# Last layer's output stage: ScalarE scales every fourth chunk, GpSimd the other three

## What is computed

```
def _L3_conv_ref(z, ...):
    zn = _layernorm(z, ln_in_w, ln_in_b)
    a = jax.nn.sigmoid(zn @ Wga + bga) * (zn @ Wla + bla)
    b = jax.nn.sigmoid(zn @ Wgb + bgb) * (zn @ Wlb + blb)
    k = jnp.einsum('bimc,bmjc->bijc', a, b)
    out = jax.nn.sigmoid(zn @ Wgo + bgo) * (_layernorm(k, ln_o_w, ln_o_b) @ Wlo + blo)
    return out

x = x + _L3_conv_ref(_gn(x), ...)
```

## Time and profile before

| what | value |
|---|---|
| median of three executions | 2137.73 us (2136.56 to 2138.88) |
| profiled execution, its own time | 2139.81 us |
| its span in the trace | 2137.9 us |
| mean granted clock of PE, share of full speed | 0.961 |
| busy in the whole span: PE, DVE, ACT, POOL | 1773.6, 1526.9, 1309.6, 806.5 us |
| output stage of layer 3 | about 1985 us to the end |

### The profile page before, as it was taken

How to read it: one execution, slowest core, us unless ns; L and a number is a source line. 1 busy time by engine, 2 the same in 40 slices (tenths; PEclk the granted TensorE clock), 3 DMA queues, 4 the chain that set the end, 5 groups by cost and what they waited for, 6 DMA issues and landing times. The chain is left out here.

```text
span 2137.9 us, 40855 instructions
## 1 busy us (share of the span) xinstructions
PE 1773.6 (83%) x10389; PEld 1036.9 (48%) x10389; DVE 1526.9 (71%) x3171; ACT 1309.6 (61%) x2413; POOL 806.5 (38%) x740
## 2 busy tenths in 40 slices
PE   0899996797998999965699799877699997799665
PEld 0345444685553454543355476633344444588332
DVE  7588886126754999996876487488588889344775
ACT  0587884466995878754599576433378876344322
POOL 0045445006980444445799100188100000000799
PEclk9999998898999999998899899999899999899999
DMA  7367776775994456546499687299547877753799
GB/s 319 124 201 232 243 240 208 276 308 180 362 368 144 139 166 188 166 139 239 156 367 363 223 292 239 68 389 403 191 143 232 247 225 228 255 235 157 254 352 338
DMA packets 336161, 512.92 MB, mean 240 GB/s; under 512 B 23851, under 2 KB 189486, under 8 KB 329654
## 3 DMA queue, kind: packets, MB, share of 16 engines
q1 hardware_dynamic: 336054, 511.71, 69.4%
HBM read 293.51 MB, written 205.52 MB: 233 GB/s over the span
## 5 line engine op out<-in xcount | busy, mean ns | idle before, releaser
L1300 POOL TENSOR_TENSOR shared<-O,out_rs 128x128 f32<-128x128 f32 (+1 forms) x128 | 91.6, 718 | 678.2 <-DVE out_rs L1207 677.1
L599 PE MATMUL ps<-w_heads,hi 64*128 64x256 f16 x3072 | 290.8, 272 | 33.8 <-DVE sig L750 21.7
L662 ACT ACTIVATE sig<-ps,largest 128x512 f32<-128x512 f32 x384 | 247.3, 691 | 52.1 <-PE ps L599 49.3
L1097 ACT ACTIVATE O<-ps 128x512 f32 (+1 forms) x144 | 151.6, 1053 | 190.4 <-PE ps L1018 190.4
L1344 PE MATMUL ps<-ident,shared 128*128 128x128 f32 (+1 forms) x1024 | 162.9, 284 | 106.8 <-POOL shared L1300 106.7
L1344 PEld LDWEIGHTS ps<-ident,shared 128*128 128x128 f32 (+1 forms) x1024 | 114.2, 133 | 277.0 <-POOL shared L1300 192.2
L599 PEld LDWEIGHTS ps<-w_heads,hi 64*128 64x128 f16 x3072 | 154.0, 94 | 187.9 <-DVE sig L750 71.5
L643 ACT ACTIVATE zs<-ps,shift 128x512 f32<-128x512 f32 x192 | 131.8, 686 | 184.0 <-PE ps L567 183.8
L599 PE MATMUL ps<-w_heads,lo 64*128 64x256 f16 x1536 | 212.4, 270 | 0.0
L750 DVE SCALAR_TENSOR_TENSOR sig<-ps,largest,sig 128x512 f32<-128x512 f32 x256 | 179.6, 741 | 37.9 <-ACT sig L662 36.4
L567 PE MATMUL ps<-xs,center 128*128 128x512 f32 x384 | 202.8, 610 | 1.0 <-DVE shift L347 1.0
(11 more groups left out here) (156 smaller groups left out, 3718.6 us busy)
## 6 DMA issues: line engine op xcount, KB each, us to landing
shared<-left_right SPq DMA_DIRECT2D x34, 2048.0 KB, 12.1
shared<-gate SPq DMA_DIRECT2D x256, 256.0 KB, 4.5
gate<-gates SPq DMA_DIRECT2D x96, 512.0 KB, 2.9
x_dram<-shared SPq DMA_DIRECT2D x192, 256.0 KB, 4.3
shared<-x_dram SPq DMA_DIRECT2D x192, 256.0 KB, 4.6
xs<-x_dram SPq DMA_DIRECT2D x64, 512.0 KB, 4.2
left_right<-stage SPq DMA_DIRECT2D x64, 448.0 KB, 5.8
left_right<-shared SPq DMA_DIRECT2D x64, 448.0 KB, 5.8
```

The source lines that it names most:

```text
L599: last = pe.matmul(PAIR[row][:, g, kb * S:kb * S + S], tokens[half, q % 8, at:at + P], k["w_heads"][half, part, :], start=(step == 0), sto ...
L662: act.activation(sig[:, slot, :].rearrange("p (c e) -> p c e", c=4), pair(row, 0), ACT.Sigmoid, scale=k["largest"][:, 0:1]).then_inc(c["si ...
L1097: act.activation(o_of(ch), ps[h % 4 // 2][:, h % 2, :].rearrange("p (b g i) -> p b g i", b=2, g=2), ACT.Copy).then_inc(c["o_copied"].sem, 1)
```

## The change

In layer 3 alone (`shares_scale = n == 3`) the chunks whose number has remainder 3 modulo 4 are no longer scaled by POOL. ACT scales them, in a new `scale`: eight activations of 128x64, one for each group of tokens, with function Copy and the token's reciprocal as the per-partition scale operand. ACT does this for chunk q+4 right after its `copy` of chunk q+3. A new counter `act_scaled` tells PE when such a chunk is ready and DVE when the reciprocals may be overwritten; POOL's counter `scaled` now counts three chunks in four. Everything else, and layers 0 to 2, stay as they are.

```
--- before.py
+++ after.py
@@ -91,7 +91,7 @@
             "fold_vec", "fold_mm", "fold_act", "stat_done", "z_done", "sq_done", "var_done", "log_done", "r_done", "r_part", "r_split", "spread_done",
             "xn_done", "hi_done", "lo_done", "proj_done", "gate_mm_done", "sig_done", "gate_done", "masked", "lr_done", "pair_read",
             "tr_done", "tr_copied", "tri_done", "packed", "o_copied", "o_stored", "o_moved",
-            "ln_stat", "ln_root", "ln_scale", "centered", "scaled", "wt_done", "wt_copied", "gated",
+            "ln_stat", "ln_root", "ln_scale", "centered", "scaled", "act_scaled", "wt_done", "wt_copied", "gated",
             "out_mm_done", "u_cleared", "out_gated", "x_new", "counted", "aggregated")}
 
         for n, ring in (("const_in", 1), ("x_in", 8), ("lr_out", 2), ("first_out", 2), ("gate_out", 4), ("lr_in", 2),
@@ -1122,6 +1122,7 @@
     STAT, CENTER, SCALE, TURN, GATED, OUTMM, OUTGATED = BATCH + 6, 5, 4, 3, 2, 1 if gate_first else 2, 1
     LOAD_X, LOAD_G = 4, 6 if gate_first else 5
     RING = 4
+    shares_scale = n == 3
     with ExitStack() as ctx:
         def sb(name, shape, dt=F32):
             return ctx.enter_context(nc.sbuf_tensor(f"out_{name}_{n}", shape, dt))
@@ -1142,6 +1143,16 @@
             at = q % BATCH * 2 * ROWS
             return values[:, q // BATCH % BATCHES, :, at:at + 2 * ROWS, :].to_broadcast([P, 2, 2 * ROWS, H])
 
+        def scaled_by_act(q):
+
+            return shares_scale and q % BATCH == BATCH - 1
+
+        def scaled_by_pool(i, q):
+
+            if shares_scale:
+                return c["scaled"]((i * BATCHES + q // BATCH) * (BATCH - 1) + q % BATCH + 1)
+            return c["scaled"](i * BODY + q + 1)
+
         def bodies_of(eng, step):
 
             with eng.Fori(0, bodies - 1) as i:
@@ -1203,7 +1214,10 @@
                 batch = i * BATCHES + b
                 dve.wait_ge(c["ln_root"].sem, c["ln_root"](batch + 1))
 
-                dve.wait_ge(c["scaled"].sem, c["scaled"](batch * BATCH - (BATCHES - 1) * BATCH))
+                freed = batch - (BATCHES - 1)
+                dve.wait_ge(c["scaled"].sem, c["scaled"](freed * (BATCH - 1 if shares_scale else BATCH)))
+                if shares_scale:
+                    dve.wait_ge(c["act_scaled"].sem, c["act_scaled"](freed))
                 dve.reciprocal(rs[:, b % BATCHES].rearrange("p b t -> p (b t)"), std[:, b % BATCHES]).then_inc(c["ln_scale"].sem, 1)
                 dve.wait_ge(c["ln_scale"].sem, c["ln_scale"](batch + 1))
 
@@ -1313,7 +1327,7 @@
             def step(i, q, more):
                 if gate_first and more(CENTER):
                     center(i, q + CENTER)
-                if not gate_first and more(SCALE):
+                if not gate_first and more(SCALE) and not scaled_by_act(q + SCALE):
                     scale(i, q + SCALE)
                 if gate_first:
                     if more(SCALE):
@@ -1328,14 +1342,18 @@
                         scale(0, q - (CENTER - SCALE))
             else:
                 for q in range(SCALE):
-                    scale(0, q)
+                    if not scaled_by_act(q):
+                        scale(0, q)
             bodies_of(pool, step)
 
         @block.tensor
         def _(pe):
             def turn(i, q):
                 m = i * BODY + q
-                pe.wait_ge(c["scaled"].sem, c["scaled"](m + 1))
+                if scaled_by_act(q):
+                    pe.wait_ge(c["act_scaled"].sem, c["act_scaled"](i * BATCHES + q // BATCH + 1))
+                else:
+                    pe.wait_ge(c["scaled"].sem, scaled_by_pool(i, q))
                 free = c["gated"] if gate_first else c["wt_copied"]
                 pe.wait_ge(free.sem, free(m - 3))
                 for row in range(ROWS):
@@ -1386,6 +1404,18 @@
                     ins = act.activation(u[0:HH, q % RING], TURNED[q % 4], ACT.Copy)
                 ins.then_inc(c["wt_copied"].sem, 1)
 
+            def scale(i, q):
+                m = i * BODY + q
+                act.wait_ge(c["ln_scale"].sem, c["ln_scale"](i * BATCHES + q // BATCH + 1))
+                act.wait_ge(c["wt_done"].sem, c["wt_done"](m - 3))
+                for jb in range(2):
+                    for token in range(2 * ROWS):
+                        tokens = rows[:, jb, bass.ds(m * 2 * ROWS + token, 1), :].rearrange("p t h -> p (t h)")
+                        at = q % BATCH * 2 * ROWS + token
+                        last = act.activation(scaled[:, q % RING, jb, token, :], tokens, ACT.Copy,
+                                              scale=rs[:, q // BATCH % BATCHES, jb, at:at + 1])
+                last.then_inc(c["act_scaled"].sem, 1)
+
             def root(i, b):
                 batch = i * BATCHES + b
                 act.wait_ge(c["ln_stat"].sem, c["ln_stat"](batch * BATCH + BATCH))
@@ -1397,6 +1427,8 @@
             def step(i, q, more):
                 if more(TURN):
                     copy(i, q + TURN)
+                if more(SCALE) and scaled_by_act(q + SCALE):
+                    scale(i, q + SCALE)
                 if gate_first:
                     m = i * BODY + q
                     act.wait_ge(c["out_mm_done"].sem, c["out_mm_done"](m + 1))
@@ -1415,6 +1447,8 @@
                 act.wait_ge(c["u_cleared"].sem, c["u_cleared"](1))
             for q in range(TURN):
                 copy(0, q)
+            if shares_scale:
+                scale(0, SCALE - 1)
             bodies_of(act, step)
 
     for s in range(RING):
@@ -1427,7 +1461,10 @@
         c[name].advance(batches)
     if gate_first:
         c["aggregated"].advance(5)
-    for name in ("ln_stat", "scaled", "wt_done", "wt_copied", "out_mm_done", "x_new",
+    c["scaled"].advance(NCH - batches if shares_scale else NCH)
+    if shares_scale:
+        c["act_scaled"].advance(batches)
+    for name in ("ln_stat", "wt_done", "wt_copied", "out_mm_done", "x_new",
                  *(("centered", "gated") if gate_first else ("out_gated",))) + (("counted",) if counted else ()):
         c[name].advance(NCH)
 
```

## The result

| | before | changed |
|---|---|---|
| median of four executions each | 2137.62 us (2136.56 to 2138.88) | 2125.49 us (2124.29 to 2126.74) |
| profiled execution | 2139.81 us | 2126.74 us |
| its span | 2137.9 us | 2124.9 us |

The ratio is 0.9943, with a 95% interval of 0.9926 to 0.9960: 12.1 us less, 9 to 16 by the interval. The forecast was 2123.9 us, 13.8 less. A second set of executions of the changed kernel gave 0.9937 (0.9924 to 0.9950). Three executions in the whole series, of 2469, 2483 and 4650 us, lie far outside the others and are left out of all medians and ratios here.

The account below looks back on a forecast made before the run. POOL was taken to bound layer 3's output stage. Profiled 2139.8 us, less 15.0 for freed spacings, plus 1.2 for transfers, gives 2126.0; the median lies 2.1 below the profiled one, so 2123.9, range 2121.0 to 2130.5.

Parts of the forecast that it names:

- POOL sets the pace: Layer 3's output stage: POOL is busy 120.00 of 120 us, 2.23 us a chunk, and stays slowest after the change.
- 15 spacings of 1.00 us: POOL, layer 3's output stage: 15 of ACT's 16 chunks each free one multiplication spacing of 1.00 us, 15.0 in all.
- the last additions: End of layer 3's output stage: POOL's four back-to-back additions, 4.93 us from 2128.20, were to stay as they are.
- Transfers cost 1.2 us: Layer 3's output stage: imperfect meshing with transfers costs 0.02 us on each of 60 chunks; bounds 0 and 3.2 us.
- Eight activations take 1.6 us: ACT's scaling of one chunk: 7 spacings of 0.17 us plus a last activation of 0.39; bounds 1.35 and 3.1.
- the loop: PE's transposes, ACT's copy and scaling, then three PE steps: 6.9 us per four chunks, under POOL's 7.92.
- The threshold at which the loop decides: The loop through ACT becomes the pace and the change loses once eight activations need more than 3.6 us.
- the rival of the slow activations: Activations of 0.50 us each make the loop 9.3 us; 15 fours lose 0.4 each, 6 us, 2143.7; 4 in 100.
- PE gets denser work: PE in layer 3's output stage: full clock is granted in the stage before and work gets denser, so nothing changes.
- The limit of 358 GB/s: Skill's limit for HBM transfers of a core; the stage, at 354, would gain nothing, 2137.7 us; rival's chance 5 in 100.
- layer 2's rate of 398 GB/s: Layer 2's output stage, same three transfers per chunk: its rate shows the new pace of 397 GB/s is just possible.

Follow-up runs that it names:

- 16 columns of x: Changed kernel whose loads of x in the last output stage bring 16 of 512 columns: 2124.0 us, ratio 0.9930.
- twelve: Changed kernel with four extra activations, into an unread buffer, ahead of the eight at each of ACT's chunks: 2144.9 us, ratio 1.0025.
- the sixteen activations: Changed kernel with eight extra activations, into an unread buffer, ahead of the eight at each of ACT's chunks: 2172.3 us, ratio 1.0150.
- the filling: The sixteen activations, with PE also multiplying constants while it waits for ACT: 2154.7 us with twenty matmuls, 2142.6 us with fourteen.

## Why the prediction was right

- **POOL sets the pace: right.** The kernel before with a third of its transfers gone had the same time, and less or earlier work on ACT changed nothing.
- **15 spacings of 1.00 us: right, 14.2 arrived in the steady part.** From the start of the first addition to that of chunk 60 the kernel before took 132.7 us (1996.75 to 2129.4, the second of the four at 2128.20). The prediction took these four for the last additions; in the kernel before one more comes after them:

```profile
2134.16 1.26 POOL L1311 TENSOR_TENSOR shared<-shared 128x512 f32<-128x512 f32 x1 [1.03 <-DMA out<-shared]
```

In the changed kernel the same stretch, to chunk 60, takes 118.4 us, as POOL's timeline shows:

```profile
1997.14 1.26 POOL L1325 TENSOR_TENSOR shared<-shared 128x512 f32<-128x512 f32 x1 [1.43 <-DVE shared L1238]
...
2011.16 1.27 POOL L1325 TENSOR_TENSOR shared<-shared 128x512 f32<-128x512 f32 x1 [0.38 <-DMA out<-shared]
...
2115.59 1.27 POOL L1325 TENSOR_TENSOR shared<-shared 128x512 f32<-128x512 f32 x1 [0.16 <-DMA out<-shared]
2117.53 1.27 POOL L1325 TENSOR_TENSOR shared<-shared 128x512 f32<-128x512 f32 x1 [0.67 <-DMA out<-shared]
2119.82 2.54 POOL L1325 TENSOR_TENSOR shared<-shared 128x512 f32<-128x512 f32 x2 [1.02 <-DMA out<-shared]
```

- **Transfers cost 1.2 us: near in size, half in another place.** The whole was 15.0 - 13.4 = 1.6. In the steady part two waits for stores, 0.38 and 0.16, make 0.5; another 0.2 lies in one pair of additions (2.67 instead of 2.50 us) for which the profile names no cause. The last additions, which the prediction had left as they were, cost another 0.8: from the start of chunk 60 to the end of the last one it was 6.0 us and is 6.8, with 1.7 us of waits for stores instead of 1.0; with 16 columns of x they took 6.0 again. Stores landed after 4.9 us, as expected, instead of 4.3.
- **The remainder of the span.** 14.2 - 0.8 is 13.4; the stage's first addition came 0.4 later after the program's start, in stages that weren't changed. That is the 13.0 us between the spans. The medians moved 12.1; what they differ from 13.0 is within the interval.
- **Eight activations take 1.6 us: too small.** They take 2.00, spaced by (2.00 - 0.336)/7 = 0.24 instead of 0.17. The step that failed is the one from duration to spacing: of the 0.09 by which the per-partition operand lengthened a 128x512 activation I carried only 0.02 over to the spacing, and no row gave the spacing of 128x512 activations without the operand. At 64 elements the spacing is the whole 0.09 above L923's, 0.24 instead of 0.15, while the duration rose from 0.30 only to 0.34. L923 writes in another pattern, so that the operand alone makes the difference isn't shown. The Trainium skill, "ScalarE: Activation LUTs", section "What ACT_TABLE_LOAD costs", puts an activation at 186 ns plus 0.833 for each element, with 93 more for each pointer operand, and lets two in a row overlap by 93. Estimated from this page, one takes 332 ns and the spacing is 239, and the trace agrees with 336 and 238. The error cost nothing here, because the loop came to 7.3 instead of 6.9 us under POOL's 7.9.
- **The threshold at which the loop decides: right at full clock, wrong in what follows.** Activations of 3.6 us were to be the point from which the change loses. With 3.0 (twelve, 0.96 above the 2.00 of the eight) the time was already above the kernel before. The loop with twelve at full clock is 8.2 as computed; what the rival of the slow activations left out is that PE, waiting longer, then also works at half its clock. The sentence that PE gets denser work and nothing changes in its clock held for the changed kernel, with a wait of 1.81 us in each four, and not much beyond it. That the change stayed on the safe side was in part luck, since the prediction gave no thought to what the new wait does to the clock.
- **The limit of 358 GB/s: no limit here.** This stage ran at 394 GB/s in the changed kernel and at 405 with half the chunks on ACT. The Trainium skill, "DMA: Bandwidth & Descriptors", section "Where 436 GB/s comes from", gets its 358 as half of what two cores have together. This program runs on one core, and the measurement decides.

## What to carry over

When an engine that sets the pace hands work to another, work out the loop that the handing over closes, and not only the other engine's load: ACT had 3.4 of 7.9 us free, and 1 us more in its place in the order cost more than the whole gain. Moving work off the pace-setter pays until the next limit, and a stretch elsewhere in the same trace with the same transfers shows where that lies: layer 2's rate of 398 GB/s told that hardly anything would be left beyond a fourth of the chunks, and half of them on ACT brought nothing measurable. A DMA share of one doesn't show that transfers are the limit: here it stood at 1.01 while a third fewer bytes changed nothing in the pace, and another stage with the same transfers ran at a higher rate.

## What was not expected of the hardware

A longer wait of PE cost more than its own length here, by the granted clock. With a wait of 1.81 us in each four chunks it stayed at 1.00; with 2.7 it was 0.88 over the stretch and with 3.7 it was 0.82, and the first step after the wait took 2.61 us instead of 1.30. For the sixteen activations the clock was worth 27 of 44 us by the ratios, or 30 of 47 by the medians, as the filling showed. Of two equal waits of 2.69 us one was followed by slow steps and the other not; why is open. The eight activations of 128x64 with a per-partition scale lasted 0.336 us each and followed one another every 0.24 us.
